# A 128-row mixing kernel, unread matmuls from the first microsecond, and one of eight groups of a scaling moved from GpSimd to VectorE

## What is computed

```python
# layer 0
h   = gelu(cond @ W0 + b0); h = gelu(h @ W1 + b1)
att = softmax(h @ W2 + b2)                              # (64 samples, 8 kernels)
agg_w = einsum('bk,koi->boi', att, weight[..., 0])      # a 64x64 matrix for each sample
mixed = einsum('boi,bih->boh', agg_w, x) + (att @ bias_k)[:, :, None]
x = x + fp8_matmul(mixed, ffn_weight) + ffn_bias        # both operands scaled by their largest |value|
# layer 1
y = grouped_conv1d(x, conv_weight, K=9, groups=4) + (cond @ c_weight.T)[:, :, None] + fside
Wd = (W_q.reshape(N, 8, 128).astype(float16) - zero[:, :, None]) * scale[:, :, None]
x = x + y @ Wd.reshape(N, 1024).T + bias
```

## Time and profile before

| | |
|---|---|
| median of 3 runs | 531.62 us (531.44 to 533.4) |
| the profiled execution | 531.13 us, of which the span of instructions is 529.0 us |
| PE busy | 514.0 us (97%) |
| DVE busy | 412.5 us (78%) |
| ACT busy | 246.7 us (47%) |
| POOL busy | 57.1 us (11%) |

### The profile page before, as it was taken

The page is one execution under the profiler, slowest core; times in us unless marked ns, Lnnn a source line. Parts: engine busy times, 40 slices in busy tenths (PEclk is TensorE's granted clock), DMA queues, the critical chain, the costliest instruction groups (busy, mean ns, idle before and its releaser), DMA issues.

```text
span 529.0 us, 9379 instructions
## 1 busy us (share of the span) xinstructions
PE 514.0 (97%) x3433; PEld 284.4 (54%) x3465; DVE 412.5 (78%) x518; ACT 246.7 (47%) x284; POOL 57.1 (11%) x66
## 2 busy tenths in 40 slices
PE   6899989899999999999999999999999999999997
PEld 4345444355555555555555555555555555555563
DVE  7579999887877777777777777777777777777652
ACT  3669987665344444444444444444444444442310
POOL 4247665011000000000000000000000000000000
PEclk9999999999999999999999999999999999999999
DMA  8998292145676666665556655656555666666532
GB/s 281 396 402 307 105 371 84 40 121 124 198 184 185 197 184 185 185 180 180 180 180 180 180 180 180 180 180 180 180 180 180 182 183 180 183 187 187 195 120 81
DMA packets 85075, 100.02 MB, mean 189 GB/s; under 512 B 34324, under 2 KB 66518, under 8 KB 85062
## 3 DMA queue, kind: packets, MB, share of 16 engines
q1 hardware_dynamic: 84178, 99.02, 59.2%
q0 software_dynamic: 512, 0.63, 0.7%
q10 hardware_dynamic: 372, 0.20, 0.2%
HBM read 58.41 MB, written 32.75 MB: 172 GB/s over the span
## 4 chain that ended last, share of the span: by engine, by line
PE 84%; DVE 10%; issue 2%; ACT 2%; ACTq 0%; DVEq 0%
PE pair L1160 42%; PE pair L1134 19%; PE pair L1150 16%; DVE stat L789 6%; PE pair L1035 2%; PE pair L1124 1%; ACT work L554 1%; DVE work L719 1%; DVE work L804 1%; PE pair L1022 1%; DVE Y L804 1%; DVE work L722 1%; PE pair L1112 0%; DVE Y L862 0%; PE pair L986 0%
## 5 line engine op out<-in xcount | busy, mean ns | idle before, releaser
L1160 PE MATMUL pair<-f1T,work 128*128 128x512 f16 x1024 | 231.0, 379 | 0.0
L1160 PEld LDWEIGHTS pair<-f1T,work 128*128 128x128 f16 x1024 | 98.8, 98 | 113.6
L596 ACT ACTIVATE work<-Y,consts 128x1024 bf16 (+1 forms) x29 | 33.3, 1148 | 186.2 <-DVE work L883 186.2
L902 DVE TENSOR_TENSOR work<-Y,work 128x512 f16<-128x512 f16 (+1 forms) x64 | 71.2, 1119 | 46.4 <-ACT work L629 45.4
L1134 PE MATMUL pair<-f0T,work 128*128 128x512 bf16 x435 | 98.6, 379 | 1.5
L1150 PEld LDWEIGHTS pair<-taps,work 128*128 128x128 f16 x1536 | 88.4, 98 | 7.8 <-issue 0.4
L1150 PE MATMUL pair<-taps,work 128*128 128x128 f16 x1536 | 91.0, 219 | 0.0
L915 DVE TENSOR_TENSOR Y<-pair,Y 128x512 f32 (+1 forms) x64 | 43.9, 686 | 44.3 <-PE pair L1160 44.3
L629 ACT CAST work<-Y 128x512 f16 (+1 forms) x64 | 69.5, 1138 | 17.7 <-DVE Y L892 15.6
L1134 PEld LDWEIGHTS pair<-f0T,work 128*128 128x128 bf16 x464 | 45.4, 98 | 54.8
L1035 PE MATMUL pair<-Y,work 128*128 128x512 f32 x128 | 61.3, 621 | 3.5 <-DMA Y<-in_x_dram 1.7
(11 more groups left out here) (147 smaller groups left out, 241.7 us busy)
## 6 DMA issues: line engine op xcount, KB each, us to landing
Y<-in_x_dram SPq DMA_DIRECT2D x64, 512.0 KB, 3.9
out_dram<-Y SPq DMA_DIRECT2D x31, 512.0 KB, 3.8
split_rows<-work SPq DMA_DIRECT2D x30, 520.0 KB, 2.7
work<-split_rows SPq DMA_DIRECT2D x30, 520.0 KB, 3.9
Y<-in_L_ffn_weight_dram SPq DMA_DIRECT2D x8, 512.0 KB, 6.9
Y<-in_L_ffn_W_q_dram SPq DMA_DIRECT2D x5, 512.0 KB, 13.4
work<-in_L_ffn_W_q_dram SPq DMA_DIRECT2D x3, 512.0 KB, 14.8
work<-work SPq DMA_DIRECT2D x8, 65.0 KB, 3.5
```

Source lines behind the costliest of these rows:

```text
L902: nc.vector.tensor_tensor(split[:, r, s, 1], v[:, r, :], split[:, r, s, 0], ALU.subtract)\
L1160: last = mm(ps[2 + h][:, :], y1s[n][:, e, k, :], f1T[:, k, h * H:(h + 1) * H], start=False, stop=(e == 1 and k == KT - 1), skip_group_chec ...
```

## The change

1. `KC` is 16 and `KR` 128: the mixing matmuls contract over 128 rows. There are still four, of 512 columns each. `attM` is made in two instructions of 512 columns each on DVE, and the first matmul waits for the first of them. The copies out of PSUM now write runs of 16 adjacent values instead of values 8 apart. `wkf` is loaded by four DMAs of 128 pieces of 256 bytes each on POOL's queue, where it was one DMA on ACT's.
2. POOL makes `ident` first, then issues these four DMAs, then the two of `convraw`.
3. ACT issues the loads of `mw2` and `rowb` after its copy `embT`, and makes `ident_b` and `ident_h` after the exponential.
4. DVE clears `idle_rows` first. PE runs five unread matmuls of 512 columns on it before anything else, two of 128 columns in the perceptron, 16 as before (now on `idle_rows`) and eight more ahead of the mixing matmuls. All the turns of tap rows come after the mixing matmuls.
5. On DVE the reductions `largest_w0(0)` to `(2)` stand behind `attM` and ahead of `place_last`, `largest_w0(3)` behind it.
6. `times_w1` on POOL does seven of the eight groups; the eighth is a new DVE instruction `times_last(r)`, after `largest_mixed(2r+1)` and ahead of `largest_mixed(2r+2)`. PE's turn waits for both.

```diff
@@ -80,11 +80,11 @@
         def mix_src(m, par, b):
-            return pair[m][par * C:(par + 1) * C, :].rearrange("p (q c t b) -> p b t q c", q=2, c=KC, t=T)[:, b]
+            return pair[m][par * C:(par + 1) * C, :].rearrange("p (c t b) -> p b t c", c=KC, t=T)[:, b]
         def mix_dst(m, par, b):
-            rows = mixw[b * C:(b + 1) * C, :, b * C:(b + 1) * C]
-            return rows.rearrange("p t (c m q o) -> p m o t q c", c=KC, m=2, q=2)[:, m, par]
+            o = b * C + (2 * m + par) * KC
+            return mixw[b * C:(b + 1) * C, :, o:o + KC]
         def held(eng, value):
@@ -106,11 +106,12 @@
         mixw = work[:, 0:T * P].rearrange("p (t m) -> p t m", t=T)
-        KC = C // K
+        KC = P // K
         KF = C * C // KC
         KR = K * KC
         wkf = work[0:KR, 5 * L:5 * L + KF]
         attM = work[0:KR, 6 * L:6 * L + KC * B].rearrange("p (c b) -> p c b", c=KC)
+        idle_rows = f1T[:, 0, 0:H]
         wide_taps = f0T[:, 0, 0:CG * R8 * 4].bitcast(fp32).rearrange("p (c j) -> p c j", c=CG)
         tapsf = slot(21)
         taps_rows = slot(22).rearrange("p (w c r) -> p w c r", w=R8, c=CG)
@@ -123,8 +124,8 @@
         embT, ctwT = mlp[:, 512:576], mlp[:, 576:704]
         h0T, h1T = mlp[:, 704:768], mlp[:, 768:832]
         mw2 = mlp[:, 832:840]
-        attR = mlp[0:B, 848:848 + KR]
-        own_c = mlp[0:KR, 912:912 + KC]
+        attR = mlp[0:B, 840:840 + KR]
+        own_c = mlp[0:KR, 996:996 + KC]
         rowb = mlp[0:1, 976:984]
         mb0, mb1 = (f0T[0:1, R8 - 2, n * 2 * P:(n + 1) * 2 * P].bitcast(fp32) for n in range(2))
         ex = mlp[0:B, 986:994]
@@ -437,13 +440,16 @@
         @block.gpsimd
         def _(pool):
-            for b in range(NB):
-                pool.dma_start(convraw[b * C:(b + 1) * C], convw).then_inc(ld["convw"], 16)
             nc.gpsimd.memset(ident[:, :], 0.0).then_inc(ident_zero, 1)
             nc.gpsimd.memset(ones, 1.0).then_inc(ones_made, 1)
             pool.wait_ge(ident_zero, 1)
             nc.gpsimd.affine_select(out=ident[:, :], in_=ident[:, :], compare_op=ALU.not_equal, fill=1.0, base=0,
                                     pattern=[[-1, P]], channel_multiplier=1).then_inc(ident_made, 1)
+            wk_rows = cwk.rearrange("k (o c) i a -> o k c (i a)", c=KC)
+            for o in range(C // KC):
+                pool.dma_start(wkf[:, o * C:(o + 1) * C], wk_rows[o]).then_inc(ld["wk"], 16)
+            for b in range(NB):
+                pool.dma_start(convraw[b * C:(b + 1) * C], convw).then_inc(ld["convw"], 16)
             nc.gpsimd.memset(mbk2, 0.0).then_inc(mbk_zero, 1)
             nc.gpsimd.memset(wide_taps, 0.0).then_inc(taps_zero, 1)
             nc.gpsimd.memset(tapcols, 0.0).then_inc(tapcols_made, 1)
@@ -472,7 +478,9 @@
             def times_w1(n):
                 pool.wait_ge(zs_ev, 1)
                 pool.wait_ge(w1_less, n + 1)
-                nc.gpsimd.tensor_tensor(grp(w1c(n)), grp(w1c(n)), wide(scale_of(n)), ALU.mult).then_inc(w1d, 1)
+                g = slice(0, NG - 1)
+                nc.gpsimd.tensor_tensor(grp(w1c(n))[:, g], grp(w1c(n))[:, g], wide(scale_of(n))[:, g], ALU.mult)\
+                    .then_inc(w1d, 1)
             def round_w0(r):
                 if r >= 2:
@@ -529,15 +537,12 @@
             row = lambda a: a.rearrange("(a n) -> a n", a=1)
             act.dma_start(mw1, cw1).then_inc(ld["mw1"], 16)
             act.dma_start(mb1, row(cb1)).then_inc(ld["mw1"], 16)
-            act.dma_start(mw2, cw2).then_inc(ld["mw2"], 16)
-            act.dma_start(rowb, row(cb2)).then_inc(ld["mw2"], 16)
-            act.dma_start(wkf, cwk.rearrange("k (c o) i a -> (k c) (o i a)", c=KC)).then_inc(ld["wk"], 16)
             act.wait_ge(ident_made, 1)
             nc.scalar.activation(gelu_probe, ident[:, 0:1], ACT.Gelu).then_inc(ident_cast, 1)
             act.wait_ge(mlp_mm, 1)
             nc.scalar.copy(embT, ps[0][:, 0:B]).then_inc(mlp_ev, 1)
-            nc.scalar.copy(ident_b, ident[:, :]).then_inc(ident_cast, 1)
-            nc.scalar.copy(ident_h, ident[:, :]).then_inc(ident_cast, 1)
+            act.dma_start(mw2, cw2).then_inc(ld["mw2"], 16)
+            act.dma_start(rowb, row(cb2)).then_inc(ld["mw2"], 16)
             act.wait_ge(mlp_mm, 2)
             nc.scalar.activation(h0T, ps[1][:, 0:B], ACT.Gelu).then_inc(mlp_ev, 1)
             act.wait_ge(mlp_mm, 3)
@@ -545,6 +550,8 @@
             act.wait_ge(mlp_ev, 4)
             nc.scalar.activation(ex, ps[3][0:B, 0:K], ACT.Exp, bias=nmax, accum_out=rsum).then_inc(mlp_ev, 1)
+            nc.scalar.copy(ident_b, ident[:, :]).then_inc(ident_cast, 1)
+            nc.scalar.copy(ident_h, ident[:, :]).then_inc(ident_cast, 1)
             act.wait_ge(mixw_zero, 4)
             for m in range(2):
@@ -730,6 +737,7 @@
             def clear_mixw(n):
                 nc.vector.memset(mixw[:, n * R8:(n + 1) * R8, :], 0.0).then_inc(mixw_zero, 1)
+            nc.vector.memset(idle_rows, 0.0).then_inc(idle_zero, 1)
             clear_mixw(0)
             clear_mixw(1)
             dve.wait_ge(ident_made, 1)
@@ -751,7 +759,6 @@
             dve.wait_ge(mlp_mm, 4)
             nc.vector.tensor_reduce(nmax, ps[3][0:B, 0:K], AX.X, ALU.max, negate=True).then_inc(mlp_ev, 1)
-            largest_w0(0)
             dve.wait_ge(mlp_ev, 5)
             nc.vector.reciprocal(rinv, rsum).then_inc(mlp_ev, 1)
             dve.wait_ge(mlp_ev, 6)
@@ -759,8 +766,11 @@
                                     ex.unsqueeze(2).to_broadcast([B, K, KC]), rinv, None, ALU.mult).then_inc(mlp_ev, 1)
             dve.wait_ge(mlp_mm, 5)
             dve.wait_ge(own_made, 1)
-            nc.vector.tensor_tensor(attM, ps[6][0:KR, 256:256 + B].unsqueeze(1).to_broadcast([KR, KC, B]),
-                                    own_c.unsqueeze(2).to_broadcast([KR, KC, B]), ALU.mult).then_inc(mlp_ev, 1)
+            for h in range(2):
+                c = slice(h * KC // 2, (h + 1) * KC // 2)
+                nc.vector.tensor_tensor(attM[:, c], ps[6][0:KR, 256:256 + B].unsqueeze(1).to_broadcast([KR, KC // 2, B]),
+                                        own_c[:, c].unsqueeze(2).to_broadcast([KR, KC // 2, B]), ALU.mult)\
+                    .then_inc(mlp_ev, 1)
             def scales(inv, mul, src, step):
@@ -803,9 +813,17 @@
                 zero = zero_of(n).unsqueeze(2).to_broadcast([P, NG, L // NG])
                 nc.vector.tensor_tensor(grp(w1c(n)), grp(w1i(n)), zero, ALU.subtract).then_inc(w1_less, 1)
-            for r in range(1, 4):
+            def times_last(n):
+
+                dve.wait_ge(w1_less, n + 1)
+                at = w1c(n)[:, (NG - 1) * (L // NG):]
+                nc.vector.tensor_tensor(at, at, scale_of(n)[:, NG - 1:NG].to_broadcast([P, L // NG]), ALU.mult)\
+                    .then_inc(w1d_last, 1)
+
+            for r in range(3):
                 largest_w0(r)
             place_last()
+            largest_w0(3)
             for r in range(4, R8):
                 largest_w0(r)
             dve.wait_ge(w_red, R8)
@@ -825,6 +843,7 @@
                 less_w1(r)
                 if r:
                     largest_mixed(2 * r + 1)
+                times_last(r)
                 largest_mixed(2 * r + 2)
             for n in range(2 * R8 + 1, NGRP):
                 largest_mixed(n)
@@ -980,17 +999,20 @@
         def _(pe):
             mm = nc.tensor.matmul
-            def keep_clock(n):
+            def keep_clock(n, cols=P):
                 for _ in range(n):
-                    mm(ps[7][:, 0:P], ident_b, ident_b, start=True, stop=True)
-
+                    mm(ps[7][:, 0:cols], idle_rows[:, 0:P], idle_rows[:, 0:cols], start=True, stop=True)
+
+            pe.wait_ge(idle_zero, 1)
+            keep_clock(5, H)
             pe.wait_ge(ident_made, 1)
             pe.wait_ge(ld["emb"], 16)
             nc.tensor.transpose(ps[0][:, 0:B], emb, ident[0:B, 0:B]).then_inc(mlp_mm, 1)
             pe.wait_ge(ld["mw0"], 32)
             pe.wait_ge(ones_made, 1)
             mm(ps[1][:, 0:B], mb0, ones[0:1, 0:B], start=True, stop=False)
+            keep_clock(2)
             pe.wait_ge(mlp_ev, 1)
             mm(ps[1][:, 0:B], mw0, embT, start=False, stop=True).then_inc(mlp_mm, 1)
             pe.wait_ge(ld["mw1"], 32)
@@ -1001,7 +1023,6 @@
             mm(ps[3][0:B, 0:K], ones[0:1, 0:B], rowb, start=True, stop=False)
             pe.wait_ge(mlp_ev, 3)
             mm(ps[3][0:B, 0:K], h1T, mw2, start=False, stop=True).then_inc(mlp_mm, 1)
-            pe.wait_ge(ident_cast, 2)
             keep_clock(16)
             pe.wait_ge(mlp_ev, 7)
             nc.tensor.transpose(ps[6][0:KR, 256:256 + B], attR, ident[0:B, 0:B]).then_inc(mlp_mm, 1)
@@ -1015,15 +1036,17 @@
                 if w == R8 - 1:
                     last.then_inc(taps_mm, 1)
-            turned_tap_rows(range(0, 3))
-            pe.wait_ge(ld["wk"], 16)
-            pe.wait_ge(mlp_ev, 8)
-            for q in range(4):
-                last = mm(ps[q][:, :], wkf[:, q * 2 * C:(q + 1) * 2 * C], attM.rearrange("p c b -> p (c b)"),
```

(21 more changed lines are left out.)

## The result

The changed kernel takes 540.63 us (median of 4, 539.9 to 541.37) against 532.04 us for the kernel before: a ratio of 1.017 (95% interval 1.0147 to 1.0193). The profiled execution took 541.37 us with a span of 539.5 us, 10.5 us more than the 529.0 before.

A forecast was written before the change was run, and what follows sets the result against it. It took TensorE to bound the steady part, untouched, and GpSimd to set the length of VectorE's rounds in the head. 531.1 (profiled execution) + 9.3 (rounds) - 0.9 (head) = 539.5 us, range 526 to 543.

The forecast's parts named there:

- VectorE is held, and for a whole instruction: Rounds: `times_last` waits until POOL's multiplication ends; rounds 1 to 6 each 1.17 us longer, 9.3 us in sum.
- Nothing hides it: After round 7: DVE still has eleven microseconds of reductions that must all be done, so the 9.3 us count in full.
- The small loads come late: Head: `convraw` lands at 9.1 us, `nmax` starts at 9.7 instead of 7.57, 2.1 us late; `mw2` and `rowb` similarly late.
- The table: Head: the exponential's table is already loaded when `nmax` ends, giving back 0.6 us; mixing starts at 12.0.
- The copies: Head: ACT's six PSUM copies stay at 1.08 us per 512 columns, with 0.59 as the bound.
- The clock: Head: TensorE reaches its full pace 4.4 us after the mixing matmuls start; two of them take the old 3.85 us.
- VectorE does not hold the head up: Head: DVE's two copies end at 20.2 and its five reductions at 26.2, before the first three tiles' passes at 27.6.
- The head in sum: Head: the first three tiles' passes end at 27.6 instead of 28.52, 0.9 us earlier; bounds 5.8 earlier to 2.7 later.
- rival 1: Rounds: `times_last` is not held or comes ahead of POOL's multiplication; 529.0 us, range 523.2 to 532.6; chance 0.27.
- the best head: Head's best bound: `convraw` at 7.6, full clock and short copies, DVE then deciding at 22.7; 5.8 us earlier.
- rival 2: Rounds and head: the wait is paid but the head gains its full 5.8 us; 534.6 us; chance 0.12.
- rival 3: Rounds and head: the wait is paid and small transfers queueing behind large ones make the head 2.7 us late; 543.1; chance 0.08.

The follow-up runs named there:

- e3: Changed kernel with `times_last` moved behind the one-tile reduction `largest_mixed(2r+2)`; 532.54 us, 1.0014 of the kernel before.
- e4: Changed kernel with `times_last` directly behind `less_w1` in every round, ahead of both reductions; 544.5 us in its one run.
- e1: Changed kernel without item 6: POOL multiplies all eight groups again, `times_last` is gone, the head stays changed; 531.98 us, 1.001 of the kernel before.
- e2: Kernel before with item 6 alone (eighth group on DVE as `times_last`); 541.46 us, 1.018 of the kernel before.
- e6: e5 with the small loads issued early and the four `wkf` pieces on SyncE's queue; 529.82 us, 0.9957 of the kernel before.
- e7: e6 with the eighth group on ScalarE, as an activation ahead of `keep_w0`; 529.01 us, 0.9946 of the kernel before.
- e9: e7 with thirty-two instead of sixteen unread matmuls in front of the last maxima; 527.59 us, 0.9933 of the kernel before.
- e10b: e7 with six more unread matmuls at each of three places behind the last maxima; 527.2 us, 0.9909 of the kernel before.
- e11: e7 without the five wide, two and eight early unread matmuls at the start; 527.86 us, 0.9932 of the kernel before.
- e8: Changed kernel plus thirty-two unread matmuls in TensorE's wait in front of the last maxima; 539.45 us, 1.0156 of the kernel before.
- e5: e1 plus sixteen unread 128-column matmuls in TensorE's wait in front of the last maxima; 532.41 us, 1.0018 of the kernel before.

## Why the prediction was right, step by step

The sum had two terms, 9.3 us for the rounds and -0.9 for the head, 8.4 together. The profiled executions differ by 10.2 us in time and 10.5 in span: 8.7 in the rounds, -0.3 in the head, and 2.1 behind the last reduction, where the sum had nothing. The two terms are off by 0.6 us in opposite directions, and cancel; what is missing is the third.

- **VectorE is held, and for a whole instruction.** Right, in place and size. The changed kernel ends `times_last` 0.15 us after L482; e3 and e4 move it and it moves with POOL. The terms: rounds longer by 1.17 us (measured 1.11, 8.17 - 7.06), the end of the first 16-bit step of round 1 at 39.3 (measured 38.88), 9.3 us in sum (8.7 measured). By rounds: 6.6 in rounds 1 to 6 (7.0 forecast), 0.5 in round 0 (7.59 us from L814 to L814 instead of 7.08; 0.7 forecast), 1.6 in the last (1.6).
- **Nothing hides it.** Right: e1 without the instruction is back at the kernel before, e2 has it all.
- **The small loads come late.** Right in kind, mis-sized. I took 9.1 us for the convolution weights, with 10.6 as the bound, from a landing time of 5.6 us; DMAs there took 5.7 to 6.3 us, and they arrived at 11.1. `rowb` took 7.3 us and came last (11.6). `nmax` came 4.8 us late, not 2.1. The profile's page of DMA issues gives landing times of one moment; here it was the longest that counted, since three small loads all had to be there.
- **The table.** The 0.6 us that it gives back did not arrive. The sixteen unread matmuls behind the perceptron hold TensorE until the turn of `attR` at 14.09, although VectorE has finished `attR` at 13.42, and the eight new ones stand on the chain behind it (0.97 us). `nmax` to mixing matmuls takes 2.96 us; the kernel before took 2.90, the forecast 2.3.
- **The copies.** I kept 1.08 us with 0.59 as the bound; measured 0.58. The PSUM reads are still 64 values apart, so what is left as the cause is the writes, 8 values apart before and adjacent now; no run changes them alone. That is 3.0 us won on the path.
- **The clock.** I put the full pace 4.4 us after the mixing matmuls start. In the changed kernel weight loads come 0.86 us apart before and 0.43 after about 16.9 us, only 1.6 us after the mixing matmuls begin at 15.33. That wins 1.0 us more than forecast. How long the full pace takes is not a constant of these kernels: e6, e7, e9 and e10b issue the same work up to the mixing matmuls at 10.13 and reach it at about 13.4, 11.5, 10.9 and 12.6 us. e11, without the early unread matmuls, reaches it at about 15.7, later than all four, so the early ones may be what brings it sooner; one profile has it so.
- **VectorE does not hold the head up.** Wrong, and it is the step that took the gain. Its five reductions ended at 27.0, not at 26.2, and with the first tile's behind them it took up TensorE's turn 0.84 us after that was done (28.38 against 27.54).
- **The head in sum.** -0.3 us where -0.9 was forecast comes of five terms that partly cancel: +2.7 for the loads, +0.6 for the table, -1.0 for the clock, -3.0 for the copies and about +1.3 for VectorE and the passes, each against its forecast. That the total is close is luck. The rounds are not.
- **Not foreseen:** the clock falls behind the last reductions. With DVE late, TensorE idles there for 2.9 us, and by the profile of e8 about 1.2 us of the extra 2.1 us come from it. The other 0.8 us of e8 against the kernel before I cannot place; the waits for the transfers of the split tiles are the nearest candidate and no run isolates them. In the profile of e1 the same fall hid 1.7 of the head's 2.0 us.
- **A slip in the sum of rival 1:** its range with the best head begins at 531.1 - 1.2 - 5.8 = 524.1, not at 523.2. It changes nothing in the forecast.
- **Rival 1** (not held, or ahead of POOL) fell with the first timeline. **Rivals 2 and 3** had the head at -5.8 or +2.7 us. Each had a part of the truth: the loads were later than rival 3 bounds them, the copies were as short as rival 2 has them. e6 shows what the head does without the late loads: the first mixed tile comes at 17.4, and then it waits for x.

## What to carry to other kernels

Before moving a piece of work from GpSimd to VectorE, look at what GpSimd is doing at the moment when the piece will come up. Here a VectorE instruction with two SBUF inputs waited out GpSimd's whole instruction, in every place where it was put. A piece of 0.2 us of work (an estimate from L804's length; it was never seen alone) took 1.68 us in seven rounds and 2.10 in one. The same piece at the end of the round cost nothing that can be told from zero, and on ScalarE the rounds became 0.2 us shorter. A small load that is issued behind large ones can take far longer than its size says: `rowb`, eight values, took 7.3 us from 4.26 on, with the DMA share at 1.0, and in e6, issued earlier, it was not waited for. A gain on one engine's path ends where another engine becomes the later one, as VectorE did in this head. And a gain in one stage can be taken back by the clock of the next one: after a change, look at the granted clock of the stretch behind it, and at that of several executions, for it differs between them.

## What the runs showed of the hardware that was not expected

- A copy of 64x512 float32 from PSUM with reads 64 values apart takes 1.08 us when its SBUF writes are 8 values apart and 0.58 us when they come in runs of 16, on ScalarE; on VectorE 1.08 and 0.70 us.
- TensorE's granted clock was lowered behind the last reductions in the profiles of the changed kernel, e1, e2, e3, e5, e6, e7 and e11 (lowest stretches of 3 us 0.51 to 0.66), with 1.4 to 2.9 us of idle time or sixteen unread matmuls ahead of it. It read 1.00 there in the kernel before, e4, e8, e9 and e10b, though e4 and the kernel before have no unread matmuls there, and in e4, e9 and e10b it was lowered elsewhere. In the kernel before it was lowered in 12 of 63 executions by the mean. What decides it stays open.
- In the kernel before, the clock column reads 1.00 while passes come 0.86 us apart at the start. The pace of the rows, not that column, tells which level TensorE runs at in the first 25 us.
